# Node products of a four-network graph kernel: groups unrolled and software-pipelined, GpSimd's input copy removed

## What is computed

```python
# network 1, three layers
m = relu(concatenate([x[src], x[dst], ew]) @ edge_W[l] + edge_b[l])   # x @ the two 64x64 parts: per node
x = relu(concatenate([x, segment_sum(m, dst)]) @ node_W[l] + node_b[l])
# network 2
h0 = relu(x @ W_enc + b_enc)
hW = einsum('nd,rdo->rno', h0, W_rel)                                 # 8 relations
out = h0 + relu(segment_sum(hW[etypes, src], dst) + h0 @ W_self + bias)
# network 3, twice
h = relu((segment_sum(h[src], dst) / deg) @ Wl + b + h @ Wr)
# network 4, two layers
s_h, s_t = (einsum('mhd,hd->mh', tanh(h @ W), att) for W, att in ((W_h, att_h), (W_t, att_t)))
...                                                                   # attention over edges, three spreads
ent = Z.reshape(n, 128) @ W_o[l] + ent
```

## Time and profile before

| | |
|---|---|
| median of 3 runs | 13,492.65 us (13,489.85 to 13,514.09) |
| span of the profiled execution | 13,453.0 us |
| TensorE busy | 11,137.4 us (83%) |
| TensorE weight loads busy | 9,882.7 us (73%) |
| VectorE busy | 10,911.2 us (81%) |
| ScalarE busy | 5,227.5 us (39%) |
| GpSimd busy | 2,409.1 us (18%) |
| the 18 calls of `linear`, first to last instruction | 761.10 us |

### The profile page before, as it was taken

The page is one execution under the profiler, slowest core; times in us unless marked ns, Lnnn a source line. Parts: engine busy times, 40 slices in busy tenths (PEclk is TensorE's granted clock), DMA queues, the critical chain, the costliest instruction groups (busy, mean ns, idle before and its releaser), DMA issues. The chain is left out here.

```text
span 13453.0 us, 456368 instructions
## 1 busy us (share of the span) xinstructions
PE 11137.4 (83%) x106911; PEld 9882.7 (73%) x106912; DVE 10911.2 (81%) x40164; ACT 5227.5 (39%) x19100; POOL 2409.1 (18%) x7659
## 2 busy tenths in 40 slices
PE   3555399899899599976665879999998789999998
PEld 3444388799798499975553339999997338999998
DVE  6545399688688288876565999999997999999998
ACT  1000022122222022235452338865453337875454
POOL 2777300000000000001110001112221001222222
PEclk9999999899899599999896999999998999999999
DMA  1111177444243011113231554432221554432222
GB/s 54 47 50 47 45 228 236 138 128 128 80 128 115 4 41 41 41 50 88 71 87 51 148 140 115 115 92 73 70 73 47 143 147 113 115 98 73 70 73 61
DMA packets 1206840, 1232.94 MB, mean 92 GB/s; under 512 B 218352, under 2 KB 1042801, under 8 KB 1206107
## 3 DMA queue, kind: packets, MB, share of 16 engines
q1 hardware_dynamic: 1180954, 1228.47, 32.8%
q0 software_dynamic: 25792, 3.35, 0.2%
HBM read 1115.06 MB, written 116.16 MB: 92 GB/s over the span
## 5 line engine op out<-in xcount | busy, mean ns | idle before, releaser
L993 DVE TENSOR_SCALAR hot<-iota_row,place 128x128 f32<-128x128 f16 (+1 forms) x9000 | 1818.8, 269 | 158.5 <-PE acc L1092 135.7
L1711 ACT ACTIVATE msgs<-G,share 128x64 f32<-128x64 f32 x6000 | 1395.6, 315 | 1346.0 <-PE G L1725 1346.0
L985 DVE TENSOR_SCALAR hotT<-idx,iota_col 128x512 bf16<-128x512 f16 x4500 | 1323.8, 352 | 524.4 <-PE G L1138 492.1
L1725 PE MATMUL G<-u_b,hotT 128*128 x12000 | 1592.2, 276 | 50.3 <-DVE hotT L1659 50.3
L1735 PE MATMUL S<-msgs,hot 128*128 128x128 f32 x12000 | 1586.3, 275 | 0.0
L1157 ACT CAST msgs<-G 128x384 bf16<-128x384 f32 x2250 | 1020.4, 480 | 1372.7 <-PE G L1138 1368.1
L1725 PEld LDWEIGHTS G<-u_b,hotT 128*128 128x128 f32 x12000 | 1467.4, 193 | 51.0 <-issue 51.0
L1735 PEld LDWEIGHTS S<-msgs,hot 128*128 128x128 f32 x12000 | 1462.3, 192 | 0.0
L1080 PE MATMUL G<-table_m,hotT 128*128 x9000 | 1309.8, 248 | 93.4 <-issue 69.3
L1110 ACT ACTIVATE msgs<-sums 128x128 f32<-128x128 f32 x2250 | 699.3, 311 | 1762.3 <-DVE sums L1102 1400.5
L1547 ACT ACTIVATE msgs<-G,msgs 128x64 f32<-128x64 f32 x6000 | 1315.5, 333 | 30.5 <-issue 21.0
(11 more groups left out here) (323 smaller groups left out, 19877.9 us busy)
## 6 DMA issues: line engine op xcount, KB each, us to landing
idx<-pos_rows SPq DMA_DIRECT2D x6375, 128.0 KB, 2.9
hotT<-hots_d SPq DMA_DIRECT2D x750, 256.0 KB
hots_d<-hotT SPq DMA_DIRECT2D x375, 256.0 KB, 3.4
key_b<-key_rows SPq DMA_DIRECT2D x62, 416.0 KB
ty_b<-type_rows SPq DMA_DIRECT2D x62, 416.0 KB
rows<-rel_rows SPq DMA_DIRECT2D x1500, 6.0 KB
ew_now<-ew_rows_d SPq DMA_DIRECT2D x1125, 3.0 KB
sorted_d<-recs,place POOLq DMA_INDIRECT x806
```

Source lines behind the costliest of these rows:

```text
L985: op = eng.tensor_scalar(hotT[:, c % deep, n], idx[:, c, r], p.col[:, first:first + 1], None, ALU.is_equal)
L993: op = eng.tensor_scalar(hot[:, c % 2, q], p.row16[:], place[:, c % 2, q:q + 1], None, ALU.is_equal)
L1711: op = eng.activation(msgs[:, c % 2, 2 + j // HEADS, j % HEADS * D:(j % HEADS + 1) * D], G[c % 2][1][:, j * D:(j + 1) * D], ACT.Copy, scal ...
L1725: mm = eng.matmul(G[c % 2][b][:, k * W:(k + 1) * W], hotT[:, c % 2, q * P:(q + 1) * P], table[:, ds(dst_at(at, q, 24 * W), W)], start=True ...
```

## The change

`linear` is rewritten; nothing outside it changes, and its callers pass what they passed. GpSimd has no part in it any more: TensorE turns the blocks straight from the input. The loops are gone, and all five groups are written out for each engine. `tp`, `turned` and the product tile `op` are doubled (for a call with two layers `op` was two tiles before as well). TensorE turns group g+1 before it makes the products of group g, and step k (group times layers plus layer) waits only for the eviction of step k-2. VectorE copies group g+1 ahead likewise, and copies only the `K` rows that the products read. The new function can also split a layer's output into parts (`pieces`, `rest` and the semaphores `left`, `neared`, `parted`); no caller asks for it, so that these add tiles and semaphores but no instruction.

```diff
-def linear(p, s, of, K, layers, setup=None):
+def linear(p, s, of, K, layers):
...
-        turned = p.sb("turned_x", [P, GB * P], FP32, ctx)
-        held = p.sb("held_x", [P, GB, P], FP32, ctx)
-        tp = p.ps("tp", [P, 1024], ctx)
-        op = [p.ps("op", [P, 1024], ctx) for _ in range(min(3, len(layers)))]
+        turned = [p.sb("turned_x", [P, GB * P], FP32, ctx) for _ in range(2)]
+        rest = [p.sb("rest_x", [P, GB, D], FP32, ctx) for _ in range(4)]
+        tp = [p.ps("tp", [P, 1024], ctx) for _ in range(2)]
+        op = [p.ps("op", [P, 1024], ctx) for _ in range(2)]
...
-            @block.gpsimd
-            def _(eng):
-                def step(g):
-                    if not isinstance(g, int):
-                        after(eng, pe, g + p0)
-                    eng.tensor_copy(held[:], of[:, ds(g * GB, GB), :]).then_inc(pool.h, 1)
-                step(0)
-                with eng.Fori(1, G) as g:
-                    step(g)
-                pool.at += G
-
             @block.tensor
             def _(eng):
-                with eng.Fori(0, G) as g:
-                    after(eng, pool, g + (q0 + 1))
+                def turn(g):
+                    after(eng, copied, c0 + g - 1 if g > 1 else 0)
                     for b in range(GB):
-                        mm = eng.transpose(tp[:, b * P:(b + 1) * P], held[:, b, :], p.ident[:])
-                    mm.then_inc(pe.h, 1)
-                    after(eng, v, g + (v0 + 1))
+                        mm = eng.transpose(tp[g % 2][:, b * P:(b + 1) * P], of[:, g * GB + b, :], p.ident[:])
+                    mm.then_inc(turns.h, 1)
+
+                turn(0)
+                for g in range(G):
+                    if g + 1 < G:
+                        turn(g + 1)
+                    after(eng, copied, c0 + g + 1)
                     for n, (w, bias, N, func, out) in enumerate(layers):
-                        if n >= NO:
-                            after(eng, act, g * NL + (a0 + n - NO + 1))
+                        k = g * NL + n
+                        if k > 1:
+                            eng.wait_ge(evicted.h, e0 + outs(k - 1))
+                            after(eng, left, l0 + cut(k - 1) if cut(k - 1) else 0)
                         for b in range(GB):
-                            mm = eng.matmul(op[n % NO][:, b * N:(b + 1) * N], turned[0:K, b * P:(b + 1) * P],
+                            mm = eng.matmul(op[k % 2][:, b * N:(b + 1) * N], turned[g % 2][0:K, b * P:(b + 1) * P],
                                             w, start=True, stop=bias is None)
...
-                    after(eng, act, g * NL + (a0 + NL))
...
             @block.vector
             def _(eng):
-                with eng.Fori(0, G) as g:
-                    after(eng, pe, g + (p0 + 1))
-                    eng.tensor_copy(turned[:], tp[:, 0:GB * P]).then_inc(v.h, 1)
-                v.at += G
+                def copy(g):
+                    eng.wait_ge(turns.h, t0 + g + 1)
+                    after(eng, products, m0 + (g - 1) * NL if g > 1 else 0)
+                    eng.tensor_copy(turned[g % 2][0:K], tp[g % 2][0:K, 0:GB * P]).then_inc(copied.h, 1)
...
+                copy(0)
+                for g in range(G):
+                    if g + 1 < G:
+                        copy(g + 1)
...
             @block.scalar
             def _(eng):
-                with eng.Fori(0, G) as g:
...
+                for g in range(G):
                     for n, (w, bias, N, func, out) in enumerate(layers):
-                        after(eng, mm_done, g * NL + (m0 + n + 1))
-                        eng.activation(out[:, ds(g * GB, GB), :],
-                                       op[n % NO][:, 0:GB * N].rearrange("p (b f) -> p b f", f=N),
-                                       func).then_inc(act.h, 1)
-                act.at += G * NL
+                        k = g * NL + n
+                        eng.wait_ge(products.h, m0 + k + 1)
+                        of_k = op[k % 2][:, 0:GB * N].rearrange("p (b f) -> p b f", f=N)
+                        if pieces[n]:
...
+                        else:
+                            eng.activation(out[:, g * GB:(g + 1) * GB, :], of_k, func).then_inc(evicted.h, 1)
```

More of the change, by code:

```diff
@@ new lines, in _ @@
+                copy(0)
+                for g in range(G):
+                    if g + 1 < G:
+                        copy(g + 1)
+                    for n, (w, bias, N, func, out) in enumerate(layers):
+                        k = g * NL + n
+                        for i in range(pieces[n]):
+                            j = cut(k) + i
+                            eng.wait_ge(evicted.h, e0 + outs(k + 1))
+                            after(eng, parted, d0 + j - 3 if j > 3 else 0)
+                            eng.tensor_tensor(rest[j % 4][:], op[k % 2][:, 0:GB * N].rearrange("p (b f) -> p b f", f=N)
+                                              [:, :, i * D:(i + 1) * D], out[i](g, 0), ALU.subtract).then_inc(left.h, 1)
+                        if k > 0:
+                            last_part(k - 1)
@@ L798, in _ @@
+                last_part(G * NL - 1)
+                after(eng, parted, d0 + cut(G * NL) if cut(G * NL) else 0)
             @block.scalar
             def _(eng):
[L800 to L805 removed]
@@ L806, in _, with second_part @@
-                act.at += G * NL
+                def second_part(k):
+                    for i in range(pieces[k % NL]):
+                        eng.wait_ge(left.h, l0 + cut(k) + i + 1)
+                        eng.copy(layers[k % NL][4][i](k // NL, 1), rest[(cut(k) + i) % 4][:]).then_inc(neared.h, 1)
+                for g in range(G):
+                    for n, (w, bias, N, func, out) in enumerate(layers):
+                        k = g * NL + n
+                        eng.wait_ge(products.h, m0 + k + 1)
+                        of_k = op[k % 2][:, 0:GB * N].rearrange("p (b f) -> p b f", f=N)
+                        if pieces[n]:
+                            for i in range(pieces[n]):
+                                eng.activation(out[i](g, 0), of_k[:, :, i * D:(i + 1) * D], func).then_inc(evicted.h, 1)
+                        else:
+                            eng.activation(out[:, g * GB:(g + 1) * GB, :], of_k, func).then_inc(evicted.h, 1)
+                        if k > 0:
+                            second_part(k - 1)
@@ L809, in fetch @@
+                second_part(G * NL - 1)
+        turns.at += G
+        copied.at += G
+        products.at += G * NL
+        evicted.at += outs(G * NL)
+        for x in (left, neared, parted):
+            x.at += cut(G * NL)
 def fetch(p, pairs):
```

26 lines of the change are left out of this document (17 added, 9 removed).

## The result

The changed kernel takes 13,275.74 us (median of 4 runs, 13,250.06 to 13,283.9), the kernel before on the same chip 13,494.26 (4 runs, 13,489.85 to 13,514.09): ratio 0.9831, 95% interval 0.9817 to 0.9845, 218.5 us less. The forecast was 13,284 us, in a range of 13,232 to 13,312.

What follows compares the result with a forecast made beforehand. The prediction took the 18 calls' chain of transposes, copy, products and eviction as the limit, then TensorE. Savings by kind of call summed to 209 us, taken from the 13,492.65 us median: 13,284 us, range 13,232 to 13,312.

Steps and rivals of the forecast that it cites:

- What bounds a call: In each call, a chain of transposes, copy, products and eviction, 9.52 us a group, was the limit; behind it TensorE.
- The copy: GpSimd's input copy is on the path only before each call's first transposes: 0.77 us, 18 times; later copies bring nothing.
- The loops: Writing out four loops, five turns each, saves nothing; the 0.48 us from eviction to next transposes belongs to the wait.
- Transposes ahead and their cover: TensorE transposes group g+1 before group g's products, hiding copies and evictions; without that cover, some 2 us a group again.
- The table loads: In `wht` calls, ScalarE's table reload (1.28 us) falls from five times to once; on the chain before, not counted again.
- Changes of shape: Between 128-row transposes and 64-row products: one per set, 0.29 us (0.18 for `wenc`, `wself`), none for `wn`, `w_s`, `wo`.
- C: Starting written-out instructions on the engines loses part of the gain over 90 groups: 13,421 us, at half 13,352; chance 0.07.
- D: Instruction starts on TensorE's path cost 3.0 us a group, making the kernel slower: 13,553 us; chance 0.01.
- E: A misplaced wait makes each group's products wait for the eviction before; only 14 us gained, 13,479 us; chance 0.02.
- B: TensorE's clock rises in the calls: 13,236 us if only those without bias, 13,136 if others too; chance 0.10.
- The median: Outside the profiled span: the 39.65 us by which the runs' median exceeds it stay untouched by the change, giving 13,284 us.
- Passes outside: A sign of being wrong in the main: passes outside the calls moving by more than some us.

## Why the prediction was right, step by step

The forecast saving was 209 us. The windows give 216.8 (761.10 to 544.34). Of this 5.9 is the second `wo` call's risen clock, so that at the slow clock it was 210.9: the sum held within 2 us. A part of that is luck, for its errors cancel: `wrel` and `wht` came out 4 us longer than forecast together, and `wsd`, `wn`, `w_s` and `wo` some 5 us shorter. Beside it lie two things that the prediction didn't have. Each call's end is 0.25 us shorter (from its last instruction to the next block's first 0.53 us before and 0.28 now, where two calls follow each other; the same with the copy put back and with the transposes not ahead), 4.5 us in 18 calls; and the second and third edge pass lost 1.7 and 7.7. Together some 230 us (216.3 for the calls from their first weight load on), inside the interval of 209 to 247 that the ratio gives; the medians' 218.5 and 228.9 differ from it by no more than the sorting stretch moves between executions.

**By kind of call.** Forecast and measured: `wsd` 43.2 and 42.9, `wenc` 37.2 and 37.3, `w_s` 36.9 and 36.5, `wn` 36.9 and 35.3 to 35.9 (begun on the fast clock), `wrel` 18.1 and 18.7, `wht` 28.8 and 29.4, `wo` 16.95 and 16.5. No kind of call is off by more than 0.7 us at the slow clock.

**What bounds a call.** The reading of the group as a chain, with TensorE next behind it, held: with transposes ahead, nothing but TensorE's own work is left in the windows.

**The copy.** 0.77 us at the front of each call, nothing for the later copies: measured 0.75 to 0.77.

**The loops.** Here the prediction was wrong, and it didn't show in the sum. It held that the 0.48 us between eviction and transposes goes with the wait. It goes with the loop (or, in part, with the second wait in it, for GpSimd's copy): the same wait for the eviction, written out, takes 0.05. Since the change removes both, the terms were only shared out wrongly: writing out brings 43 us, not nothing, and the transposes ahead 154 instead of 196. A version that kept the loops and turned one step ahead would have been given too short a time by this argument; it wasn't run.

**Transposes ahead and their cover.** Held, but the prediction gave the evictions' cover too high a price. It said that without it "it would be some 2 us a group again". With one product tile, P(g) waits for the eviction before it, and calls of one layer lose only 0.7 to 1.2 us each: the transposes ahead cover an eviction by themselves.

**The table loads.** Two of 1.28 us instead of ten, both at the start of a call under the first transposes. The prediction called them "on the chain". They weren't: where transposes still wait for evictions, `wht` gains 2.9 us from the copy and the writing out, like the other calls with their 3.0 to 3.1. No term rested on it.

**Changes of shape.** One of 0.29 us was taken for each set of transposes. The timeline of `wrel` shows two: products of 2.13 us start 2.43 before the transposes behind them (0.30), and transposes of 1.07 start 1.27 before the products (0.20), 0.50 together. Three sets make 0.6 us more a call than forecast, which is what `wrel` and `wht` are above it. It lay within the bounds of nothing to 0.58 a set.

**The rivals.** C and D didn't happen: in the timelines of `wrel` and `wht` no wait inside a call that ended by "issue" is above 0.33 us, the changes of shape, and writing out brought 43 us instead of costing. E was excluded by the windows, and it was priced wrong. As it is worded, with P(g) waiting for the eviction before it, it is the kernel with one product tile: its calls take 571 us, and of the gain of 216 us 190 is left, not 14. Only with the transposes behind the evictions as well does most of it go, and even then the time was 13,426 and not 13,479, since the loops were gone too.

B came true in part: the clock rose in one of eight calls without bias in the first trace and in two in the second, 5.9 and 12.4 us of the 48. The prediction set `wht`'s 64-row bursts against it, and for those it stayed right: no `wht` call rose. It said nothing of what decides between calls of the same kind. `wrel` rose once and stayed down seven times in two traces, with the same instructions throughout, so it isn't the code of the call alone; with the copy back the second `wo`, whose transposes come 0.77 us later, didn't rise. That points to when the call begins; it wasn't tested by itself. The Trainium skill ("TensorE: Matmul & The Clock Gate", PE-mode transpose) says that transposes don't count as busy in the same way. The `wrel` call that rose doesn't bear that out clearly: ten transposes are over half of the 3.66 us ahead of the rise. In the experiment with 128 rows all `wrel` and `wht` calls rose, but its `wenc`, `wself` and `w_s` calls, with 128 rows as well, did not, so what decides stays open.

**The median.** That 39.65 us above the span are untouched by the change gave the right time for a wrong reason, and that is luck. They were no fixed part outside the span (that is 1.8 us): the profiled execution was a short one, in the sorting and in the fourth network's passes.

**Passes outside.** "If passes outside them move by more than some us" was named as a sign of being wrong. One moved by 7.7 us. The empty blocks move it by as much, so the likely cause is the place of the code.

## What to carry to other kernels

A short block that stands alone between barriers is priced from its own window: once its groups are turned ahead, its time is TensorE's instructions plus one start and one tail, and that sum was good to 1%, single calls to 4%. After it, count what TensorE still does: changing the number of rows between instructions cost 0.2 to 0.3 us each time, one bias product for five blocks and zero rows up to 128 together took another 290 us from a function that the change had left at 545, more than the change itself. And before a span is compared with another, compare the stretches that the change doesn't touch: here they moved by 36 us between executions, and by 8 us with the place of the code.

## What the runs showed of the hardware that was not expected

- A turn of these loops with waits on semaphores costs about 0.54 us of hand-offs on the path, against straight code: 0.43 from eviction to the next transposes (a second wait, for GpSimd's copy, included) and 0.11 from products to eviction. Leaving a block whose engines end in loops costs 0.25 us more.
- With zero rows up to 128 in products and biases, calls are faster, not slower: at the same clock 27.2 us instead of 37.3 (`wenc`), because neighbouring instructions no longer differ in rows, and with the clock that rises 11.2 to 12.4 instead of 18.8 (`wrel`).
- A pass of 801 us is faster by 8 us with the same code behind a block of empty instructions. A difference of 0.1% between two kernels needn't come from what was changed in them.
